# Attention on one core: PV products of two steps together, with shorter and longer rings

## The reference, cut to what matters

```python
qkv = jnp.einsum('bse,ehd->bshd', x, qkv_w) + qkv_b
q, k, v = jnp.split(qkv, 3, axis=-1)
logits = jnp.einsum('bqhd,bkhd->bhqk', q, k) / 8
logits = jnp.where(mask, logits, -large)
attn = jnp.einsum('bhqk,bkhd->bqhd', softmax(logits), v)
x = x + jnp.einsum('bqhd,hde->bqe', attn, out_w) + out_b
...
x = x + shared(norm(x)) + sum over the top two experts
```

## Time and profile before

| what | value |
|---|---|
| median of 3 runs | 971.55 us (968.47 to 974.1) |
| the profiled execution | 968.54 us |
| its span | 966.7 us |
| TensorE busy | 915.7 us, 95% |
| GpSimd busy | 725.2 us, 75% |
| VectorE busy | 716.6 us, 74% |
| ScalarE busy | 701.6 us, 73% |
| heads 0 to 14 | 61 to 760 us |
| head 15 | 760 to 812 us |
| shared expert, experts, output | 812 to 967 us |

### The profile page before, as it was taken

How to read it: one execution, slowest core, us unless ns; L and a number is a source line. 1 busy time by engine, 2 the same in 40 slices (tenths; PEclk the granted TensorE clock), 3 DMA queues, 4 the chain that set the end, 5 groups by cost and what they waited for, 6 DMA issues and landing times.

```text
span 966.7 us, 25810 instructions
## 1 busy us (share of the span) xinstructions
PE 915.7 (95%) x10271; PEld 757.0 (78%) x10271; DVE 716.6 (74%) x1755; ACT 701.6 (73%) x877; POOL 725.2 (75%) x457
## 2 busy tenths in 40 slices
PE   7889999999999999999999999999999979879991
PEld 6558888888888888888888888888888766449991
DVE  5978797879786978887787869786878355646665
ACT  3038878888888888888888888888788965235661
POOL 1228889898888888888988898888788978454441
PEclk8779999999999999999999999999999999999996
DMA  3321344544544454445440514141312305312214
GB/s 107 87 60 30 89 87 96 105 111 80 121 79 113 80 120 80 112 79 120 81 111 26 119 40 102 44 110 44 72 43 48 141 1 209 98 40 64 60 46 134
DMA packets 70228, 81.88 MB, mean 85 GB/s; under 512 B 8912, under 2 KB 54098, under 8 KB 68064
## 3 DMA queue, kind: packets, MB, share of 16 engines
q1 hardware_dynamic: 67840, 76.03, 33.2%
q0 software_dynamic: 2272, 4.22, 1.2%
HBM read 21.79 MB, written 25.20 MB: 49 GB/s over the span
## 4 chain that ended last, share of the span: by engine, by line
PE 85%; DVE 8%; ACT 2%; DMA 2%; issue 2%; SPq 0%; POOL 0%; DVEq 0%; POOLq 0%; ACTq 0%
PE bg L1203 14%; PE st L1283 13%; PE st L1284 13%; PE pv L1315 7%; PE pv L1317 7%; PE pv L1319 6%; PE bg L1193 3%; PE bg L1154 3%; PE bg L1155 2%; PE bg L1156 2%; PE bg L1213 2%; DVE row_max L981 2%; PE st L1296 2%; PE bg L1452 1%; PE bg L1443 1%
## 5 line engine op out<-in xcount | busy, mean ns | idle before, releaser
L578 POOL TENSOR_TENSOR p_lo<-prob,p_hi 128x1024 f16<-128x1024 f32 x320 | 617.2, 1947 | 135.0 <-ACT p_hi L688 133.7
L687 ACT ACTIVATE prob<-st,p_bias 128x1024 f32<-128x1024 f32 x320 | 330.0, 1031 | 119.1 <-PE st L1284 89.0
L688 ACT ACTIVATE p_hi<-st,p_bias 128x1024 f16<-128x1024 f32 x320 | 328.1, 1025 | 0.0
L981 DVE TENSOR_REDUCE row_max<-bg 128x1 f32<-128x512 f32 x384 | 255.5, 686 | 14.5 <-PE bg L1203 8.7
L1283 PE MATMUL st<-big 128*128 128x512 f32 (+3 forms) x640 | 241.9, 380 | 2.4 <-ACT p_hi L688 1.6
L1203 PE MATMUL bg<-big 128*128 128x512 f32 (+3 forms) x640 | 236.5, 399 | 4.6 <-DVE v_parts L971 2.1
L1315 PE MATMUL pv<-v_parts,p_hi 128*128 128x65 f16 x2176 | 235.1, 194 | 1.4 <-POOL p_lo L578 1.4
L1315 PEld LDWEIGHTS pv<-v_parts,p_hi 128*128 128x128 f16 x2176 | 200.1, 96 | 45.1 <-issue 32.9
L1317 PE MATMUL pv<-v_parts,p_hi 128*128 128x64 f16 x2176 | 233.9, 195 | 0.0
L1284 PE MATMUL st<-big 65*128 65x512 f32 (+3 forms) x640 | 232.5, 369 | 0.0
L1319 PE MATMUL pv<-v_parts,p_lo 128*128 128x65 f16 x2176 | 232.2, 192 | 0.0
(11 more groups left out here) (216 smaller groups left out, 1143.2 us busy)
## 6 DMA issues: line engine op xcount, KB each, us to landing
big<-big SPq DMA_DIRECT2D x192, 128.0 KB, 2.3
row_dram<-fill SPq DMA_DIRECT2D x8, 1290.0 KB, 10.8
big<-part_dram SPq DMA_DIRECT2D x8, 1088.0 KB, 8.7
big<-big SPq DMA_DIRECT2D x16, 512.0 KB, 4.3
part_dram<-stage_parts SPq DMA_DIRECT2D x32, 176.0 KB, 2.5
part_dram<-stage_parts SPq DMA_DIRECT2D x16, 192.0 KB, 3.8
stage_raw<-ffn_w SPq DMA_DIRECT2D x16, 176.0 KB, 3.0
v_parts<-row_dram SPq DMA_DIRECT2D x39, 64.5 KB, 1.8
```

Source lines behind the costliest of these rows:

```text
L578: nc.gpsimd.tensor_tensor(o, a, b, ALU.subtract).then_inc(p_lo_ready, 1)
L687: nc.scalar.activation(o32, src, ACT.Exp, bias=p_bias[:], scale=D ** -0.5)
L688: nc.scalar.activation(o16, src, ACT.Exp, bias=p_bias[:], scale=D ** -0.5).then_inc(exp_done, 1)
L981: nc.vector.tensor_reduce(row_max[:, t, c:c + 1], bank, AX_X, ALU.max).then_inc(bg_drained, 1)
```

## The change

The PV products come in pairs: an even step has none, an odd step n has those of groups n - 5 and n - 4 (`LAG` = 4). `prob` gets a ring of three groups, `p_hi` and `p_lo` rings of seven, all counted by G = 20h + n and not by n. ScalarE waits, beside the PV product of G - 7, for the low part of G - 3. The slots of the attention tasks and of head 15's tasks move to later steps, `normalise` moves by one step to m + 5, and the planner, which is not changed itself, places the max tasks anew. Four PV products instead of three are left behind step 19 of head 15. The experts' scratch moves from `prob` to the words of `p_hi`.

```diff
-PRING, STRING, BGRING = 5, 2, 3
-LAG = 3
+EXP_RING, PRING, STRING, BGRING = 3, 7, 2, 3
+LAG = 4
...
-ATT_SLOTS = ((6, 8), (10, 12), (16, 18))
-ATT_LAST = (4, 6)
-LAST_HEAD = {5: [("att_t", PAIRS - 1, 0)], 6: [("att_y", PAIRS - 1, 0)], 7: [("turn", 0)],
-             9: [("att_t", PAIRS - 1, 1), ("rows_t", 0)], 10: [("att_y", PAIRS - 1, 1)], 11: [("turn", 1)],
-             13: [("rows_t", 1)], 15: [("att_t", PAIRS - 1, 2)], 16: [("logits", 0)], 17: [("att_y", PAIRS - 1, 2)],
-             18: [("ranks", 0)], 19: [("turn", 2)]}
+ATT_SLOTS = ((8, 10), (12, 14), (17, 19))
+ATT_LAST = (6, 8)
+LAST_HEAD = {7: [("att_t", PAIRS - 1, 0)], 8: [("att_y", PAIRS - 1, 0)], 9: [("turn", 0)],
+             11: [("att_t", PAIRS - 1, 1), ("rows_t", 0)], 12: [("att_y", PAIRS - 1, 1)], 13: [("turn", 1)],
+             15: [("rows_t", 1)], 16: [("logits", 0)], 17: [("att_t", PAIRS - 1, 2)],
+             18: [("ranks", 0), ("att_y", PAIRS - 1, 2)], 19: [("turn", 2)]}
...
-        prob = sb("prob", [P, PRING, 2 * BLK], F32)
+        prob = sb("prob", [P, EXP_RING, 2 * BLK], F32)
...
-        tail = pflat[:, (SRING + HRING) * BLK:]
+        tail = high_words[:, 2 * P:]
...
                 wait(act, p_used, G - PRING + 1)
+                wait(act, p_lo_ready, G - EXP_RING + 1)
...
                     masks(n)
-                    m = (n - LAG) % NG
-                    if m < n or h:
-                        for k in range(2):
-                            p_times_v(h if m < n else h - 1, m, k)
+                    if n % 2 == 0:
+                        continue
+                    for m in ((n - LAG - 1) % NG, (n - LAG) % NG):
+                        if m < n or h:
+                            for k in range(2):
+                                p_times_v(h if m < n else h - 1, m, k)
```

More of the change, by code:

```diff
@@ L573, in p_low @@
                 pool.wait_ge(exp_done, G + 1)
-                ring = n % PRING
-                a = prob[:, ring].rearrange("p (k c) -> p k c", k=2)[:, :, lo:hi]
+                ring = G % PRING
+                a = prob[:, G % EXP_RING].rearrange("p (k c) -> p k c", k=2)[:, :, lo:hi]
                 b = p_hi[:, ring].rearrange("p (k c) -> p k c", k=2)[:, :, lo:hi]
@@ L683, in exps @@
                 wait(act, p_used, G - PRING + 1)
+                wait(act, p_lo_ready, G - EXP_RING + 1)
                 src = st[:, n % STRING, :, lo:hi]
-                o32 = prob[:, n % PRING].rearrange("p (k c) -> p k c", k=2)[:, :, lo:hi]
-                o16 = p_hi[:, n % PRING].rearrange("p (k c) -> p k c", k=2)[:, :, lo:hi]
+                o32 = prob[:, G % EXP_RING].rearrange("p (k c) -> p k c", k=2)[:, :, lo:hi]
+                o16 = p_hi[:, G % PRING].rearrange("p (k c) -> p k c", k=2)[:, :, lo:hi]
                 nc.scalar.activation(o32, src, ACT.Exp, bias=p_bias[:], scale=D ** -0.5)
@@ L1302, in p_times_v @@
                 b, p = GROUPS[n]
-                B, (i, s) = h * NB + b, divmod(h, 2)
+                B, (i, s), G = h * NB + b, divmod(h, 2), h * NG + n
                 if k == 0:
@@ L1308, in p_times_v @@
                         wait(pe, attn_ready, B)
-                    pe.wait_ge(p_lo_ready, h * NG + n + 1)
+                    pe.wait_ge(p_lo_ready, G + 1)
                 kt = 2 * p + k
@@ L1314, in p_times_v @@
                     cols = slice(k * BLK + j * P, k * BLK + (j + 1) * P)
-                    nc.tensor.matmul(out, p_hi[:, n % PRING, cols], v[:, 0:D + 1],
+                    nc.tensor.matmul(out, p_hi[:, G % PRING, cols], v[:, 0:D + 1],
                                      start=(kt == 0 and j == 0), stop=False, skip_group_check=True)
-                    nc.tensor.matmul(out[:, 0:D], p_hi[:, n % PRING, cols], v[:, D + 1:VW],
+                    nc.tensor.matmul(out[:, 0:D], p_hi[:, G % PRING, cols], v[:, D + 1:VW],
                                      start=False, stop=False, skip_group_check=True)
-                    mm = nc.tensor.matmul(out, p_lo[:, n % PRING, cols], v[:, 0:D + 1],
+                    mm = nc.tensor.matmul(out, p_lo[:, G % PRING, cols], v[:, 0:D + 1],
                                           start=False, stop=(kt == 4 * b + j), skip_group_check=True)
```

## The result

The changed kernel takes 987.83 us (median of 4 runs, 986.85 to 988.64) against 970.29 for the kernel before on the same chip: ratio 1.0175 (95% interval 1.0149 to 1.0201, given in brackets from here on), 17.5 us slower. Slower was the likeliest sign of the forecast, but 977 was the size, and its range ended at 985. The profiled execution took 988.64 us (span 986.8), 20.1 us of span more than that of before, whose profiled execution lay 1.7 us under its median.

A forecast was written before the change was run, and what follows sets the result against it. TensorE, busy in 95% of the span, was taken as the bound. Switches -10.5, ring +18.9, ScalarE +1, waits gone -1 and head 15 -1 gave +7.4, trimmed to +5.5: 977 us against the 971.55 median, range 960 to 985.

The forecast's parts named there:

- The saving (-10.5): Fewer fp32/fp16 switches on TensorE around PV blocks: 0.70 us a head, 10.5 us in fifteen heads (bounds 8.8 and 14).
- Rival 5: The load behind PV is hidden or shows elsewhere, so pairing saves nothing: 988 us; chance 2%.
- The ring (+18.9): TensorE waits for VectorE to drain three background banks: 1.5 us an even head, 1.1 an odd; bounds 9.5 and 24.
- the walk: Step-by-step placing of TensorE and VectorE tasks with durations from profile rows; held good to some 0.1 us a place.
- ScalarE (+1): Score tiles close together make ScalarE's exponentials end some 0.2 us late for step 19 of even heads: 1 us in all.
- The waits of before (-1): Some 1 us of the earlier kernel's waits goes, the old wait at the shift in even heads among them.
- The trim (-1.9): The sum of +7.4 cut to +5.5, since waits early in a head make later ones shorter.
- head 15 (-1, measured +6.1): In the last head, ScalarE's waits for scores walked from 9.1 to 8.4 us; -1 us taken, bounds -4 and +4.
- Rival 3's condition: Ring waits stay under 4 us, so the kernel is faster: 962 us; chance 21%.
- rival 2: Ring waits of about 10 us cancel the switches saved: 970 us; chance 28%.
- ScalarE's wait on low parts: ScalarE's new wait for GpSimd's low part of three groups back: done 1 us or more ahead, should not appear.
- the one place checked: Odd head of the kernel before, step 9, first maximum: 0.16 us to spare in the profile, 0.25 by the walk.

The follow-up runs named there:

- half-work kernels: The kernel before and the changed kernel, each with VectorE reading half the columns of maxima wider than 128: 960.62 us and 961.45 us.
- half-work after: The changed kernel with VectorE reading half the columns of each maximum wider than 128, TensorE's work untouched: 961.45 us, ratio 0.9909.
- list alone: The kernel before with only the new list of slots for head 15: 972.42 us over 10 runs, ratio 1.0009.

## Why the prediction was wrong in size

- **The saving (-10.5)** held. I took the waits out of the distances between the matmuls' starts in heads 1 to 13 of both traces (what a distance has beyond the plain price of its matmul, by the prices of the prediction): what is left of an even head falls from 43.75 to 43.07 us and of an odd one from 45.58 to 44.89, 0.69 us a head where 0.70 was put. A first fp32 matmul of 0.32 us stands behind a mask too, at the end of an even step, and not only at the ends of odd steps as forecast. Head 6 of after:

```profile
349.47 0.29 PE L1297 MATMUL st<-mask_cols_b,ident_b 128*128 128x128 bf16 x2
349.57 0.48 PE L1155 MATMUL bg<-xn_hi,split 128*128 128x512 f32 x1
349.89 0.39 PE L1156 MATMUL bg<-xn_lo,split 128*128 128x512 f32 x1
```

  But the second mask gives way to it after 0.03 us instead of 0.056, so the net price is some 0.057 us, as put (0.054). With half the maxima the heads keep little of this: an odd one comes out 0.4 us under before's, and 0.44 us of waits behind the attention's split are left in it; even ones keep waits for copies (2.2 us in three waits) and, ahead of step 19, 0.3 us for ScalarE.
- **Rival 5** reached nearly the time measured, 988, by luck. Its ground, a load behind PV that is hidden, is not what the trace shows: at none of the 130 ways out of a PV block in heads 1 to 13 of after does the fp32 load start ahead of the last PV matmul, and at nine in ten it starts within 0.01 us behind that matmul's start.
- **The ring (+18.9).** Mechanism, places and size were right, and the half-work kernels show that VectorE's time is the cause. In the places walked, the distances between starts in after lose 0.51, 0.31, 0.40 and 0.11 us in an even head (steps 5, 9, 11, 15; 1.33 against 1.5 walked), and 0.1, 0.43 and 0.64 in an odd one (steps 7, 8 where I had put 9, and the shift; 1.17 against 1.1). For eight even and seven odd heads that is 18.8 us. That the bank is what TensorE waits for is read from the two places above; no run changed the number of banks.
- **The first step that failed** is that the walk was taken for the whole list. Steps 3 and 4 (0.44 us, part of it single heads whose copies land late) and the scores of 15 and 19 (0.24) of even heads, and steps 6, 13 and 15 of odd ones (0.22, 0.24, 0.20), hold 0.67 us a head more, 10 us in fifteen heads, for which the sum had 1 us, given to ScalarE. About half of it is not new: an even head of before already waits 0.22 us at the start of its maxima in step 4, and heads 0 and 14 came out 0.3 us shorter than before. What is left is the gap of the heads, 13.1 - 8.4 = 4.7 us.
- **ScalarE (+1)** was right in place: the scores wait for it ten times, seven of them ahead of step 19 of even heads, 2.2 us in all.
- **The waits of before (-1).** The wait at its shift, which I gave to even heads, is there once, in head 0 (0.5 us).
- **The trim (-1.9)** had no row behind it. The reason given, that early waits shorten later ones, is not what the distances show: the walked places kept about their size and the others came on top.
- **The second step that failed is head 15 (-1, measured +6.1)**, the largest term missed, and outside its bounds of -4 and +4. I walked ScalarE's waits to 8.4 us; they came to 15.7 in the profile. The waits of TensorE for attn are not what grew. Before has two, of 3.07 us and, for the layer norm:

```profile
PE bg L1236 <- DVE attn L836: 1.9, 1, 1.9
```

  After has two as well, of 3.52 and 2.08 us:

```profile
798.90 0.63 PE L1214 MATMUL bg<-ident,attn 128*128 128x128 f32 x4 [3.52 <-DVE attn L1041]
...
811.96 0.63 PE L1237 MATMUL bg<-ident,attn 128*128 128x128 f32 x4 [2.08 <-DVE attn L837]
...
815.25 3.42 PE L1243 MATMUL bg<-gate_w,xn 128*128 128x8 f32 x16
```

  The walk had no term for the clock. Behind the second wait, from 813.3 to 823.5, it was granted at 0.50, and TensorE was busy throughout (10.20 of 10.20 us). The router's matmuls (L1243), which took 1.85 us in before, took 3.42, and ScalarE's last two waits for scores, 1.5 us together in before, came to 6.4. What the slow stretch costs can be read: the half-work after has the same instructions in head 15, and its steps 0 to 11 agree with after's to 0.02 us. It too waits 2.07 us there, but then has 3.4 us at 0.50 and not 10.2. The same two steps (16 and 17), of after and of half-work after:

```profile
813.40:823.70 10.30, 10.30 (x80) 9.36 (x78) 4.29 (x32) 4.23 (x4) 5.03 (x3) 0.51 0.01 2
```

```profile
787.70:794.10 6.40, 6.40 (x81) 5.82 (x78) 3.25 (x30) 3.86 (x4) 3.39 (x2) 0.88 0.02 4
```

  They take 3.9 us more in after, and the whole head 3.2 more. So of the 6.1 us about half went with the clock and 0.7 is the moved PV product; by subtraction some 2 us are left for the new list. That agrees with the +1 to 2 us of list alone in ten runs. It is a difference of single executions, and why the slow stretch lasted 10.2 us in one and 3.4 in the other is open. The six kernels with the old list have heads 15 of 51.6 to 53.2 us (3.4 to 6.8 us at 0.50), the seven with the new one 54.5 to 59.8 (6.8 to 17.0 us at 0.50). Single products with the new list gave the longest ones (58.4, 59.5, 59.8).
- **The moved slots** I priced only through the walk of the paired kernel. Without pairs they cost 12 us, so a forecast of each edit by itself would have had two costs of 12 us to find, and would have summed them wrongly. Why they do not add I can only argue: both push VectorE's work against the same two points, the ring's third bank and the shift in slot 18, and one delay covers the other. No run isolates that.
- **Rival 3's condition** (waits under 4 us) was far off, rival 2's as well. ScalarE's wait on low parts never shows, as put.

## What to carry to other kernels

The saving on the busiest engine was worth only what the next engine's slack allowed (0.69 us a head saved, 1.33 us of an even and 1.17 of an odd head lost in the places walked): look for the tightest moment of the ring between them, not at the share of busy time (VectorE was idle for 8 us or more of every middle head here, and at the one place checked 0.16 us from being late). If a walk is the argument, walk every slot of a period, and check the walk of before at several of them; a sum of five places is a lower bound. Halving the suspected engine's work in both kernels separates "the saving is not there" from "the saving is taken back". Read the granted clock of each stretch in every profile that is compared: a difference of some us in one stretch can go with the clock, as in steps 16 and 17 here (10.3 us at 0.51 against 6.4 at 0.88). The repeated waits of after on the ring's three banks, 21.4 us in 62 waits, went with less work for VectorE, where 1.2 us in 4 waits for row_max were left; no run tried a fourth bank.

## What the runs showed of the hardware

- Half the maxima's work made before 10 us faster in the median. The profiled executions lie 5.3 us apart (the half-work one was the slowest of its four), and all of that and more lies ahead of head 0 (5.4 us) and in its heads (3.0 us), while what comes behind is 3.1 us longer. Head 0's scores start at 55.7 us instead of 61.1. The windows of the stretch ahead, of before and of before with half the work:

```profile
0.00:61.10 61.10, 48.78 (x176) 32.70 (x176) 45.44 (x94) 9.37 (x18) 10.45 (x29) 0.76 0.30 77
```

```profile
0.00:55.70 55.70, 43.84 (x177) 30.26 (x177) 38.35 (x95) 9.37 (x18) 10.45 (x29) 0.88 0.33 84
```

  VectorE has 7.1 us less to do, and the granted clock is 0.88 instead of 0.76 (13.6 us at 0.50 instead of 29.6). Which share of the 5.4 us is the clock's was not separated.
- In head 15 of after the granted clock fell to 0.50 twice, each time behind a wait of TensorE for attn: for 3.4 us behind the one of 3.52 and for 10.2 us behind the one of 2.08. The mean of the head was 0.88 against 0.97 in the earlier trace rows, where it fell once, for 3.4 us behind the wait of 3.07, and not behind the one of 1.9.
- A single head can be longer because copies land late. In after, SyncE's row of four copies of "big" (their issues, not their transfers) ahead of head 5's maxima lasts 3.77 us against 2.42 two heads earlier, the second of them lands 4.1 us after its start against 2.4, and a maximum's matmul in head 4 (47.6 us instead of 46.7) waited for a copy of "big". Other long heads were not traced to their cause:

```profile
158.66 2.42 SPq L423 DMA_DIRECT2D big<-big  x4
...
254.16 3.77 SPq L423 DMA_DIRECT2D big<-big  x4
...
261.17 0.30 PE L1204 MATMUL bg<-big 128*128 128x128 f32 x1 [0.84 <-DMA big<-big]
```
